# Two chunks in one accumulating store in the last part of a convolution chain

## What is computed

```python
h = gelu(batchnorm(conv1x1(h, w_c2, b_c2), bn2_g, bn2_b))   # 512 channels, 128 x 128
C = h.shape[1] // 4
return haar_idwt(h[:, :C], h[:, C:2 * C], h[:, 2 * C:3 * C], h[:, 3 * C:])
...
y00 = (ll + lh + hl + hh) * 0.5      # likewise y01, y10, y11, interleaved to 256 x 256
...
x = x + _L1_conv_ref(_gn(x), ...)
```

## Time and profile before

| | |
|---|---|
| median of 3 runs | 5600.16 us (5597.89 to 5601.34) |
| the profiled execution's own time | 5600.85 us |
| its span | 5599.2 us |
| mean granted clock of TensorE | 0.945 of full speed |
| busy: TensorE matmul, VectorE, ScalarE, GpSimd | 82%, 86%, 75%, 20% |
| last part | from about 4153 us to the end |

### The profile page before, as it was taken

The page is one execution under the profiler, slowest core; times in us unless marked ns, Lnnn a source line. Parts: engine busy times, 40 slices in busy tenths (PEclk is TensorE's granted clock), DMA queues, the critical chain, the costliest instruction groups (busy, mean ns, idle before and its releaser), DMA issues.

```text
span 5599.2 us, 54191 instructions
## 1 busy us (share of the span) xinstructions
PE 4595.8 (82%) x12292; PEld 2113.4 (38%) x12292; DVE 4814.4 (86%) x4445; ACT 4173.9 (75%) x5706; POOL 1109.0 (20%) x779
## 2 busy tenths in 40 slices
PE   1889999999999999999952777777897777777775
PEld 0334444444444444444421444444552222222222
DVE  6998898988989889899649999999738888888887
ACT  4887777777777777777536777777648888888887
POOL 0000000000000000000038777777601111111111
PEclk6999999999999999999976999999999999999998
DMA  8999999999999999999962333333239999999999
GB/s 337 371 361 412 426 425 426 417 426 425 417 426 417 426 420 421 424 360 396 348 221 79 117 117 118 119 117 117 99 100 236 235 236 236 236 236 236 236 236 224
DMA packets 260905, 1627.49 MB, mean 291 GB/s; under 512 B 30768, under 2 KB 31152, under 8 KB 96944
## 3 DMA queue, kind: packets, MB, share of 16 engines
q1 hardware_dynamic: 168624, 1022.13, 46.0%
q0 software_dynamic: 36864, 268.45, 23.1%
q10 hardware_dynamic: 55296, 335.57, 14.3%
HBM read 954.94 MB, written 671.09 MB: 290 GB/s over the span
## 4 chain that ended last, share of the span: by engine, by line
PE 35%; DMA 23%; DVE 16%; POOL 11%; issue 8%; ACT 3%; DVEq 0%; POOLq 0%; ACTq 0%; SPq 0%
DMA out_x<-arena 19%; PE ps L742 13%; PE ps L730 10%; PE ps L725 9%; POOL arena L420 5%; POOL arena L425 4%; DMA arena<-in_x 4%; DVE arena L1093 3%; DVE arena L1217 2%; DVE arena L1079 2%; ACT arena L687 2%; POOL arena L406 2%; DVE arena L1108 2%; DVE ps L1206 2%; DVE arena L972 1%
## 5 line engine op out<-in xcount | busy, mean ns | idle before, releaser
L897 PE MATMUL ps<-arena,c2T 128*128 128x512 f32 x2048 | 1035.6, 658 | 379.7 <-ACT arena L680 368.6
L730 PE MATMUL ps<-arena 128*128 128x512 f32 x2048 | 965.5, 595 | 24.9 <-DVE arena L1108 24.9
L742 PE MATMUL ps<-arena 128*128 128x512 f32 x2048 | 965.0, 615 | 12.3 <-DVE small L1057 10.4
L725 PE MATMUL ps<-arena 128*128 128x512 f32 x1920 | 913.8, 598 | 43.1 <-DVE arena L1028 22.7
L406 POOL TENSOR_SCALAR arena<-arena,taps 128x1024 f32<-128x1024 f32 (+1 forms) x256 | 285.9, 1117 | 2922.8 <-ACT arena L598 2891.5
L478 ACT ACTIVATE arena<-ps,small 128x1024 f32<-128x1024 f32 x512 | 568.1, 1109 | 322.1 <-PE ps L730 321.8
L680 ACT ACTIVATE arena<-ps,small 128x512 f32<-128x512 f32 x1024 | 713.5, 778 | 105.7 <-DVE arena L1322 94.5
L1206 DVE SCALAR_TENSOR_TENSOR ps<-arena,taps,ps 128x1024 f32<-128x1024 f32 (+1 forms) x640 | 781.5, 1272 | 6.5 <-ACT ps L624 5.8
L897 PEld LDWEIGHTS ps<-arena,c2T 128*128 128x128 f32 x2048 | 406.2, 207 | 1008.3 <-ACT arena L680 562.1
L1079 DVE SCALAR_TENSOR_TENSOR arena<-arena,shift 128x2048 f32<-128x2048 f32 x256 | 601.3, 2349 | 201.1 <-DMA arena<-in_x 139.2
L456 ACT ACTIVATE ps<-arena 128x1024 f32<-128x1024 f32 x512 | 526.3, 1028 | 169.4 <-ACT arena L478 159.5
(11 more groups left out here) (160 smaller groups left out, 5242.3 us busy)
## 6 DMA issues: line engine op xcount, KB each, us to landing
arena<-in_x SPq DMA_DIRECT2D x400, 1024.0 KB, 15.9
out_x<-arena ACTq DMA_DIRECT2D x256, 1024.0 KB, 9.0
arena<-out_x SPq DMA_DIRECT2D x256, 1024.0 KB, 16.9
out_x<-arena POOLq DMA_DIRECT2D x256, 1024.0 KB, 17.0
arena<-in_x SPq DMA_DIRECT2D x112, 1152.0 KB, 15.5
y_dram<-arena ACTq DMA_DIRECT2D x128, 512.0 KB, 8.6
arena<-y_dram SPq DMA_DIRECT2D x128, 512.0 KB, 3.2
h_dram<-arena SPq DMA_DIRECT2D x128, 512.0 KB, 2.6
```

What stands on the lines that cost most here:

```text
L725: mm(ps[:, r, :], w_right[:, :], u_buf[k][:, 2 * r:2 * r + 2, 2:W + 2], start=False, stop=False, skip_group_check=True)
L730: last = mm(ps[:, r, :], w_center[:, :], v_buf[k][:, r * BANK:(r + 1) * BANK], start=False, stop=True, skip_group_check=True)
L742: last = mm(ps[:, 4 + s % 2, :], w_c1b[:, q, :], cells[:, q // 2, q % 2, :, :], start=(q == 0), stop=(q == 3))
L897: last = mm(ps[:, 4 * k + q, :], c2T[:, q, :], h2_in[s // 2][:, k * HC:(k + 1) * HC], start=True, stop=True)
```

## The change

The four chunk buffers become two buffers of two chunks, lying side by side; `y_buf[s]` is now a half of one, so VectorE and ScalarE write the same shapes as before. GpSimd waits for both chunks of a pair and then issues one accumulating store of 2 MiB, in which each channel's row of 4096 elements is split into descriptors of 2048 elements (8192 bytes, `max_dma_last_dim=4 * CH`). There are two store semaphores instead of four, and VectorE waits for a pair's store before the pair's first chunk only.

```diff
-        y_buf = [cut(CH) for _ in range(SLOTS)]
+        y_pair = [cut(2 * CH) for _ in range(2)]
+        y_buf = [y_pair[s // 2][:, (s % 2) * CH:(s % 2 + 1) * CH] for s in range(SLOTS)]
...
-        out_stored = [sem(f"out_stored{s}") for s in range(SLOTS)]
+        out_stored = [sem(f"out_stored{s}") for s in range(2)]
...
-            for s in range(SLOTS):
-                sp.wait_ge(out_stored[s], 16 * (B * NG))
+            for k in range(2):
+                sp.wait_ge(out_stored[k], 16 * (B * NG))
...
-                    for s in range(SLOTS):
-
-                        pool.wait_ge(y_ready, b * NCH + g * SLOTS + (s + 1))
-                        pool.dma_start(out[b, :, bass.ds((g * SLOTS + s) * CH, CH)], y_buf[s],
-                                       accum_op=ALU.add).then_inc(out_stored[s], 16)
+                    for k in range(2):
+
+                        pool.wait_ge(y_ready, b * NCH + g * SLOTS + (2 * k + 2))
+                        pool.dma_start(out[b, :, bass.ds((g * SLOTS + 2 * k) * CH, 2 * CH)], y_pair[k],
+                                       accum_op=ALU.add, max_dma_last_dim=4 * CH).then_inc(out_stored[k], 16)
...
-                if not isinstance(g, int):
-                    dve.wait_ge(out_stored[s], g * 16)
+                if s % 2 == 0 and not isinstance(g, int):
+                    dve.wait_ge(out_stored[s // 2], g * 16)
```

## The result

The changed kernel takes 5768.75 us (median of 4 runs, 5766.05 to 5771.28), the kernel before 5599.43 us (4 runs). The ratio is 1.0301, with a 95% interval of 1.0289 to 1.0313: 3% slower. The forecast was 5758 us. The profiled execution took 5771.28 us with a span of 5769.7 us, 170.5 us more than the span before.

What follows compares the result with a forecast made beforehand. The prediction took the DMA engines to be full with the stores' bytes in the last part; 124 pairs x 1.18 = 146, plus 4.4, plus 7, is 157 us, on 5600.85 giving 5758 us; range 5635 to 5825.

Steps and rivals of the forecast that it cites:

- The working: Last part: a store's doubled bytes, 4.92 us, plus half a tile load, 0.62, give 5.54 against 5.55 us per chunk.
- It is a queue, not latency: Last part: most of a store's 17.3 us to landing is waiting behind other stores in full DMA engines.
- The loop: Last part, landing to landing: 10.05 + 8.3 + 4.90 + 1.30 = 24.55 us for two pairs, 1.18 us more per pair.
- The unknown: A store's time from issue to landing beyond its bytes when the queue has just run dry; taken as 3.4 us.
- The lower end: Store start costs only GpSimd's 0.857 us: loop 22.0 us, 11.0 per pair, nothing lost, 5605 us.
- the upper one: Store start costs 3.4 us plus a second 0.857: loop 25.4 us, 12.7 per pair, 5811 us.
- The ends: Last part: first store waits 4.4 us for the second chunk; four final pairs without loads add 7 us.
- (1): Last part's DMA queue never runs dry because a store's start is short when warm; 5605 us, no change; chance 0.11.
- (2): DMA queue between stores: a cost apart from bytes is saved, at most 277 us, giving 5324 us; chance 0.05.
- (3): Last part: tile loads wait longer behind two-piece rows, making TensorE late; about 170 us more, 5930 us; chance 0.05.
- Parts one and two: The kernel before its last quarter, DMA near 426 then about 117 GB/s; forecast to stay within a microsecond.

Runs made afterwards that it cites:

- the run with two buffers: The kernel before with two buffers of one chunk instead of four; 5968.26 us, ratio 1.0647.
- the earlier halving: The changed kernel, with ScalarE halving a pair's second chunk before the next chunk's gelu instead of behind it; 5687.25 us, ratio 1.0159.

## Why the prediction was right

**What bounds the kernel before.** The working, twice the bytes at 426 GB/s plus the loads, held in three ways: deeper buffers bring nothing (1.0000), 20 loads fewer bring 25.3 us (26 expected), and without loads the rate is 214 GB/s. "It is a queue, not latency" was the step on which all else rests, since a kernel bound by slot latency would have gained from eight buffers.

**The loop.** Landing to issue 10.05 forecast, 10.04 measured (10.46 in the next turn). Issue to landing 14.5 forecast, 14.7 in the median. Per pair 12.28 forecast, 12.35 measured. The DMA rate was to fall to 213 GB/s and fell to 212; VectorE was to wait some 3 us once per pair and waits 316 / 102 = 3.1.

**The unknown.** 3.4 us beyond the bytes were taken from the first store alone. The changed kernel's store without loads has 3.3 (13.1 less 9.80). The lower end, 0.86, which would have made the change free, was wrong. For the doubled descriptors I took nothing extra; the instruction grew by 0.34 us, between the two ends, 0 and 0.857. The Trainium skill's "Perfetto Trace Analysis" (section "DMA Instruction — SWDGE (GPSIMD)"), by which the profiled instruction ends when the last descriptor is written, made me call the upper one nearer; the measured growth is less than half of it. Two small errors cancel here, and to that extent the match is luck: 3.4 was too much for a store in the old form (2.8 in the shortest of the run with two buffers), and nothing for the longer instruction was too little.

**The ends.** The first store's issue, without the 3.9 us by which the whole part is late, is 4.6 us later than before; 4.4 were forecast:

```profile
4183.75 1.33 POOL L434 DMA_DIRECT2D out_x<-arena  x1 [159.00 <-ACT arena L688]
```

Without loads, at the end, the loop was to be 11.63 us per pair. From 5723.11 to 5746.24 it is 23.13 for two, 11.57:

```profile
5723.11 0.03 issue
...
5733.16 13.08 DMA out_x<-arena
5746.24 0.03 issue
```

Sum of the last part: 124 x (12.35 - 11.10) = 155, plus 4.6, plus 4 x (11.57 - 9.80) = 7, is 167 us. The span grew by 170.5, of which 3.9 lie before the part. The forecast's 157 lacked the 0.07 us per pair, 9 us; that 0.07 is within what the count can tell, so the two sums agree as well as they can be compared.

**The rivals.** (1) That the queue never runs dry did not come true with two pairs, since from a landing to the bytes of the next store it took 10.04 + 3.3 us against 11.10 in which the other pair keeps the engines busy. With four pairs exactly this rival came true, at 5602.66 us. (2) A cost per store beside its bytes: none is seen; four pairs and 128 fewer stores leave the time where it was. The Trainium skill's fixed 2.0 us per software DMA ("DMA: Bandwidth & Descriptors", "Anatomy of one DMA — SWDGE (gpsimd) path") shows here only as latency, and as 3.3 us with an accumulating store instead of 2.0; as a saving when stores are merged it does not show. (3) Starved tile loads: they took 11.3 us to landing against two chunk times of 12.35, and TensorE waited for them 31 us in all, 19 times. The kernel without any loads shows that they are not the cause.

**What was off.** The prediction has the DMA queue empty for about 1.18 us in each pair. The cost per pair is of that size, but most of it is slow first packets: a queue with no store under way makes up 18 of 1260 us, and the stores' share did not fall with the rate as forecast (88.3% after 90.8%). Parts one and two were to stay within a microsecond; the last part began 3.9 us later. I priced a tile load at 1.30 us in the loop wherever it lies. In the changed kernel it is 1.6 us (14.7 less 13.1), with the earlier halving 0.6 (13.6 less 13.0).

## What to carry to other kernels

Before merging transfers, work out two numbers: how long the engines need for the bytes that are in flight, and how long a buffer takes from landing to its next issue plus the start of a transfer in an empty queue. Merging two buffers into one makes the second number grow (here by the second chunk's compute, 5 us) while the number of buffers under way halves, and its saving per transfer is nothing where the queue was never empty. If larger transfers are wanted, keep the number of them in flight; and if the bytes are the bound, look for transfers that need not be made at all.

## What the runs showed of the hardware

- An accumulating store of 1 MiB takes 4.90 us of the DMA engines (214 GB/s of payload, in the kernel before without tile loads), twice the 2.46 that 1 MiB takes at the 426 GB/s of part one; the difference of 4.92 and 4.90 leaves nothing for a cost per store.
- Started in a dry queue, it takes more than its bytes from issue to landing: 3.4 us for the first store (1 MiB), 2.8 for the shortest one with two buffers, 3.3 for 2 MiB in the median without loads.
- Its 8192-byte packets take 0.628 us while stores stand in the queue, and up to some 1.5 us just after a restart, so a DMA share near 1 does not show that the engines move all they can.
- GpSimd's store instruction takes 0.857 us for 128 pieces of 8 KB and 1.196 for 256.
- I had not expected that the place of a 512 KB load in the loop decides between 0.6 and 1.6 us of the other queue's time.
